# A recurrent integrator on one core: state in the units of the matrix sums, and a register as ScalarE's scale

## The chip, the cores and the metric

The kernel runs on one core of a Trainium2 chip. The metric is the device time of one execution in microseconds (us).

## The reference

An attention layer makes x (8 x 512 x 1024); then x drives a network of 1024 coupled neurons in 8 batches, integrated over 512 steps with four Runge-Kutta stages each. The output is x plus the trace of q.

```python
def derivative(q, p, drive, coupling, bias):
    dq = q - q ** 3 / 3.0 - p + drive + tanh(q) @ coupling.T + bias
    dp = EPSILON * (q + ALPHA - BETA * p)
# per step: dq1..dq4 at q, q + DT/2 dq1, q + DT/2 dq2, q + DT dq3
q_next = clip(q + DT / 6 * (dq1 + 2 * dq2 + 2 * dq3 + dq4), -20, 20)   # p likewise
trace[t] = q_next
x = x + attention(x);  x = x + trace(drive=x, q0=p0=cond)
```

The steps depend on one another, and within a step each stage needs tanh of the one before it, multiplied by the whole 1024 x 1024 matrix.

## The kernel before, in words

**Layout.** The 1024 neurons lie on 128 partitions in 8 blocks; a vector of the state is a tile of 128 x 64 (8 blocks of 8 batches). All tiles of the state are pieces of one buffer, `xb`, which held x for the attention before; so the profile calls them all `xb`. The drive, 512 slices of 64 columns, stays in SBUF as `drive` and is overwritten by the result.

**The matrix.** The setup finds the power of two `power` of the largest matrix entry, divides the matrix by it (times 2**14), and keeps it as two fp16 parts, `coup`. tanh, times 4096, is likewise split into two fp16 parts, `first` and `rest`, in `tanh_parts`. So TensorE's sums come out too large by a factor that is known only at run time, through `power`. The tile `step_scale` (128 x 4) holds, for each stage, the step length divided by that factor.

**One stage** (`stage`, for s = 0 to 3; 2048 in all) is cut into two chunks of blocks, chunk 0 with 24 columns and chunk 1 with 40. TensorE does 128 small matmuls (L619): 48 that need chunk 0 of tanh, then 40 and 40 that need chunk 1. The sums of chunk 0 are complete after 88 of them, those of chunk 1 at the end. VectorE turns the sums of each chunk by a transpose (L811: 96 columns wide for chunk 0, 160 for chunk 1). `q_of` (through `axpy`, L661) multiplies the turned sums of the `rest` part by `step_scale` and adds `base`: the next stage's q. ScalarE takes tanh of it (L437), and in stages 0 and 2 also makes the `first` part (L443); in stages 1 and 3 the `first` part was made earlier from a forecast (L449, L455). VectorE's `rest_of` makes the `rest` part. TensorE starts on a chunk when both of its parts are there.

**Beside that** VectorE prepares the next `base`: `with_first_part` adds the `first` sums, again times `step_scale`; ScalarE squares q (L481); `cubic_of` (L834) and `base_of` follow. Single instructions for p, for the forecasts and for the drive are put by hand between the others. In stage 3 VectorE clips p (`clip_p`, L927) and q (`clip_q`, L941), and `drive_less_p` (L936) forms the drive minus p; `look_ahead` (L932) has added the bias to the next drive slice between the first transpose and `q_of`. In stage 1 `drive_step` (L894) takes the difference of two drive slices; in stage 2 `trace` (L947) adds q to the drive slice of the step, which is the output.

**Order.** Each engine works through its list in order, and semaphores order the engines. VectorE's and ScalarE's loops have eight stages, two steps, in their body and run some 256 times; VectorE's closes behind a stage 0. SP stores the output every 32 steps. In the code, `STEP[s]` is the step length of stage s, and a scale given as `step_scale[:, s:s + 1]` is a pointer to one value for each partition, while a Python number is a constant within the instruction.

Of the kernel before, what the change touches and what calls it, by code (L numbers as in the profile page):

```python
# [18 lines left out]
P = 128  # L19
# [71 lines left out]
UNROLLED = 2  # L91
TANH_SCALE = 4096.0
COUP_EXP = 14
DRIVE_LOADS = 8
MATRICES = 4
# [4 lines left out]
def build(nc, x, x_pt, cond, cond_p, wq, wk, wv, wo, coupling_t, bias_p, out_pt):  # L100
    ctx = ExitStack()
    with ctx:
# [9 lines left out]

        drive = sb("drive", [P, T + 2, COLS])
        steps = drive[:, 1:1 + T, :]
# [41 lines left out]
        bias_sb = sb("bias_sb", [P, NC])  # L156
        step_scale = sb("step_scale", [P, STAGES])

        states = iter(range(0, KT * N, COLS))

        def state():

            first = next(states)
            return xb[:, :, :].rearrange("p c n -> p (c n)")[:, first:first + COLS]

        q_st = [state() for s in range(STAGES)]
        q_raw = state()
# [15 lines left out]
        bias_b = state()  # L183
        drive_b = state()
        drive_p = state()
# [163 lines left out]
        @block.gpsimd  # L349
        def _(pool):  # L350

            nc.gpsimd.memset(ident[:, :], 0.0).then_inc(pool_ready, 1)
            pool.wait_ge(pool_ready, 1)
            nc.gpsimd.memset(stack[:, :, :], 0.0).then_inc(pool_ready, 1)
            pool.wait_ge(pool_ready, 2)
            nc.gpsimd.affine_select(out=ident[:, :], in_=ident[:, :], compare_op=ALU.not_equal, fill=1.0,
                                    base=0, pattern=[[-1, P]], channel_multiplier=1).then_inc(pool_ready, 1)
            pool.wait_ge(pool_ready, 3)
            nc.gpsimd.affine_select(out=stack[:, :, :], in_=stack[:, :, :], compare_op=ALU.not_equal,
                                    fill=1.0, base=0, pattern=[[-DK, P // DK], [-1, DK]],  # L360
                                    channel_multiplier=1).then_inc(pool_ready, 1)
            fills = [(wo_sum[:, :], 0.0), (ones_row[:, :], 1.0), (head_t[:, :], 0.0),
                     (q_aug[:, :], 0.0), (k_aug[:, :], 0.0), (q_aug[DK:DK + 1, :], 1.0),
                     (drive[:, 0, :], 0.0), (drive[:, 1 + T, :], 0.0)]
# [6 lines left out]
        def _(act):  # L371
# [92 lines left out]
            for j in range(NCH):  # L464
                first_part_as_now(0, j, 1)
            nc.scalar.activation(square[:, :], q_st[0][:, :], ACT.Square).then_inc(square_ready, 1)
# [189 lines left out]
        def _(dve):  # L656
# [86 lines left out]
            for c in range(NC):  # L743
# [10 lines left out]

            V.tensor_scalar(all_max[:, :], small_ps[:, 0:1], 2.0 ** -100, 2.0 ** 100, ALU.max, ALU.min)\
             .then_inc(setup, 1)
# [11 lines left out]
            last.then_inc(setup, 1)  # L768

# [13 lines left out]


            V.memset(ps[:, 0:2 * NCH, :].rearrange("p a n -> p (a n)"), 0.0)
            V.memset(tanh_parts[:, 1, :, B * REST:B * (REST + 1)], 0.0).then_inc(start_ready, 1)
            V.tensor_copy(q_st[0][:, :], cond_sb[:, :, :].rearrange("p c b -> p (c b)"))
            V.tensor_scalar(p_st[:, :], cond_sb[:, :, :].rearrange("p c b -> p (c b)"), -SHIFT, None, ALU.add)
            V.memset(z[:, :], 0.0).then_inc(setup, 1)
            dve.wait_ge(setup, 5)  # L790
            for c in range(NC):
                last = V.tensor_scalar(cols(bias_b, (c, c + 1)), cols(z, (c, c + 1)), bias_sb[:, c:c + 1],
                                       -SHIFT, ALU.add, ALU.add)
# [5 lines left out]
            V.tensor_tensor(drive_b[:, :], steps[:, 0, :], bias_b[:, :], ALU.add).then_inc(setup, 1)  # L799
            dve.wait_ge(setup, 7)  # L800
            V.tensor_tensor(drive_p[:, :], drive_b[:, :], p_st[:, :], ALU.subtract).then_inc(setup, 1)

# [127 lines left out]
            def look_ahead(at):  # L930

                V.tensor_tensor(drive_b[:, :], drive_cols[:, bass.ds(at, COLS)], bias_b[:, :], ALU.add)  # L932

            def drive_less_p(now):
                dve.wait_ge(p_ready, now)
                V.tensor_tensor(drive_p[:, :], drive_b[:, :], p_st[:, :], ALU.subtract)\  # L936
# [12 lines left out]

            dve.wait_ge(setup, 8)  # L950
            z_of_first().then_inc(setup, 1)
# [8 lines left out]
            last.then_inc(start_turned, 1)  # L960
            dve.wait_ge(setup, 9)
            dve.wait_ge(start_turned, 1)
            with_first_part(0, z_first_part, z).then_inc(setup, 1)
            dve.wait_ge(setup, 10)
            base_of(0, 1)
            g0_of()


            def stage(s, now):

# [27 lines left out]
                if s == 1:  # L998
                    q_sum_r1()
                    drive_step_of((now + 2) * (COLS // STAGES))  # L1000
                if s == 2:
                    z_without_last(now)
                    trace((now - 3) * (COLS // STAGES))
                if s == 3:
                    clip_p()
                    clip_q(made)
                    drive_less_p(now)
                rest_of(parity, 1, made)
# [77 lines left out]
```

## Time and profile before

| | |
|---|---|
| median of three runs | 5930.74 us (5926.36 to 5930.91) |
| span of the profiled execution | 5929.8 us |
| TensorE matmul, weight load | 4508.3 us (76%), 3814.4 us (64%) |
| VectorE | 5526.4 us (93%), 31560 instructions |
| ScalarE | 2595.9 us (44%) |
| VectorE, `q_of` and `with_first_part` (L661 with `step_scale`) | 1601.2 us, 6145 instructions, mean 261 ns |
| ScalarE, tanh of a chunk (L437) | 940.7 us, 4098 instructions, mean 230 ns |

The span runs from the first to the last instruction of the profiled execution; the profile gives no other time for it. The recurrence begins near 428 us. Busy time of an engine counts an instruction from its start to its end, and on VectorE the next one starts before the end of the last; so two durations are told apart in what follows, how long an instruction takes, and how long it holds its engine (from its start to the next one's).

### The profile page before, as it was taken

To read this page: it belongs to the slowest core of one execution; us is meant where nothing else is said; L and a number is where in the kernel's file an instruction comes from. 1 tells how busy PE (TensorE), PEld (TensorE's weight loads), DVE (VectorE), ACT (ScalarE), POOL (GpSimd) and SP (SyncE) were. 2 spreads that over 40 slices of the span, in tenths; PEclk is the share of its full clock that TensorE was granted. 3 is DMA by queue.
4 is the path that set the end of the run, shared out by engine and by line. 5 is a ranking of instruction groups with operands and counts; after the bars stand their busy time and mean duration, and the time that the engine had idled before them with its cause. 6 is when DMAs were issued, how large, how long until landed. Compare 5 with 4: busy or idle time off the path is not lost.

```text
span 5929.8 us, 592455 instructions
## 1 busy us (share of the span) xinstructions
PE 4508.3 (76%) x263627; PEld 3814.4 (64%) x263627; DVE 5526.4 (93%) x31560; ACT 2595.9 (44%) x12040; POOL 5.6 (0%) x16
## 2 busy tenths in 40 slices
PE   7887777777777777777777777777777777777777
PEld 3446666666666666666666666666666666666666
DVE  6569999999999999999999999999999999999999
ACT  3334444444444444444444444444444444444444
POOL 0000000000000000000000000000000000000000
PEclk9999999999999999999999999999999999999999
DMA  5100000000000000000000000000000000000000
GB/s 211 45 16 0 0 7 0 7 0 7 0 0 7 0 7 0 7 0 0 7 0 7 0 7 0 0 7 0 7 0 7 0 0 7 0 7 0 7 0 7
DMA packets 11597, 57.06 MB, mean 10 GB/s; under 512 B 2616, under 2 KB 2616, under 8 KB 8512
## 3 DMA queue, kind: packets, MB, share of 16 engines
q1 hardware_dynamic: 11056, 55.84, 2.4%
q10 hardware_dynamic: 528, 1.05, 0.0%
q8 instruction: 7, 0.11, 0.0%
q14 instruction: 6, 0.05, 0.0%
HBM read 40.11 MB, written 16.78 MB: 10 GB/s over the span
## 4 chain that ended last, share of the span: by engine, by line
DVE 44%; PE 34%; issue 11%; ACT 10%; DMA 1%; DVEq 0%; SPq 0%; ACTq 0%
PE ps L619 29%; DVE xb L661 23%; DVE turned_sums L811 10%; ACT xb L437 7%; DVE tanh_parts L661 4%; ACT tanh_parts L443 3%; DVE xb L936 2%; DVE xb L834 2%; PE ps L508 1%; DVE xb L932 1%; DVE xb L927 1%; PE ps L563 1%; PE ps L526 1%; PE ps L552 1%; PE ps L542 1%
## 5 line engine op out<-in xcount | busy, mean ns | idle before, releaser
L619 PE MATMUL ps<-coup,tanh_parts 128*16 128x96 f16 (+1 forms) x262272 | 4159.4, 219 | 1345.7 <-DVE tanh_parts L661 680.6
L619 PEld LDWEIGHTS ps<-coup,tanh_parts 128*16 128x16 f16 x262272 | 3653.2, 89 | 1852.4 <-issue 863.9
L437 ACT ACTIVATE xb<-xb 128x24 f32<-128x24 f32 (+1 forms) x4098 | 940.7, 230 | 2968.7 <-DVE xb L661 2958.5
L661 DVE SCALAR_TENSOR_TENSOR xb<-xb 128x64 f32<-128x64 f32 x11267 | 2198.2, 214 | 17.7 <-issue 0.2
L661 DVE SCALAR_TENSOR_TENSOR xb<-turned_sums,step_scale,xb 128x64 f32<-128x64 f32 (+2 forms) x6145 | 1601.2, 261 | 16.2
L811 DVE STREAM_TRANSPOSE turned_sums<-ps 128x96 f32<-128x96 f32 (+1 forms) x4096 | 1284.2, 314 | 142.2 <-PE ps L619 67.3
L661 DVE SCALAR_TENSOR_TENSOR tanh_parts<-xb,tanh_parts 128x24 f16<-128x24 f32 (+1 forms) x4098 | 712.8, 174 | 49.9
L443 ACT ACTIVATE tanh_parts<-xb 128x24 f16<-128x24 f32 (+1 forms) x2050 | 470.9, 230 | 64.5
L481 ACT ACTIVATE xb<-xb 128x64 f32<-128x64 f32 x2048 | 498.8, 244 | 0.0
L834 DVE SCALAR_TENSOR_TENSOR xb<-xb 128x64 f32<-128x64 f32 x2049 | 445.6, 217 | 0.1
L455 ACT ACTIVATE tanh_parts<-xb 128x24 f16<-128x24 f32 (+1 forms) x2048 | 357.4, 221 | 32.1
L449 ACT ACTIVATE xb<-xb 128x64 f32<-128x64 f32 x1024 | 263.2, 257 | 0.0
L407 ACT ACTIVATE probs<-ps,neg_max 128x1024 f32<-128x1024 f32 x64 | 71.4, 1115 | 145.6 <-DVE neg_max L676 145.6
L508 PE MATMUL ps<-k_aug,q_aug 128*128 128x512 f32 x256 | 126.0, 616 | 0.0
L661 DVE SCALAR_TENSOR_TENSOR drive<-ps,row_scale,drive 128x512 f32 (+1 forms) x64 | 84.2, 1349 | 41.8 <-PE ps L552 40.6
L486 ACT ACTIVATE xb<-xb 128x64 f32<-128x64 f32 x512 | 122.8, 240 | 0.0
L676 DVE TENSOR_REDUCE neg_max<-ps 128x1 f32<-128x1024 f32 x64 | 78.2, 1223 | 45.7 <-PE ps L508 45.7
L936 DVE TENSOR_TENSOR xb<-xb 128x64 f32<-128x64 f32 x512 | 115.5, 226 | 0.0
L894 DVE TENSOR_TENSOR xb<-drive 128x64 f32 x512 | 111.4, 217 | 0.0
L870 DVE TENSOR_TENSOR xb<-xb 128x64 f32<-128x64 f32 x512 | 111.2, 217 | 0.0
L947 DVE TENSOR_TENSOR drive<-drive,xb 128x64 f32 x513 | 111.0, 216 | 0.0
L941 DVE TENSOR_SCALAR xb<-xb 128x64 f32<-128x64 f32 x512 | 99.6, 195 | 0.0
(68 smaller groups left out, 792.7 us busy)
## 6 DMA issues: line engine op xcount, KB each, us to landing
xb<-in_x SPq DMA_DIRECT2D x8, 2048.0 KB, 7.9
drive<-in_x_pt SPq DMA_DIRECT2D x8, 2048.0 KB, 24.6
out_pt<-drive SPq DMA_DIRECT2D x16, 1024.0 KB, 4.5
drive<-in_coupling_t SPq DMA_DIRECT2D x8, 512.0 KB, 11.5
mask_v<-in_cond SPq DMA_DIRECT2D x8, 132.0 KB
probs<-in_wo ACTq DMA_DIRECT2D x1, 1024.0 KB, 5.5
w_qkv<-in_wq SPq DMA_DIRECT2D x1, 64.0 KB, 3.8
w_qkv<-in_wk SPq DMA_DIRECT2D x1, 64.0 KB, 5.2
```

The source lines that it names most:

```text
L437: nc.scalar.activation(cols(tanh_sb, CHUNKS[j]), cols(q, CHUNKS[j]), ACT.Tanh)\
L443: nc.scalar.activation(tanh_part(parity, j, FIRST), by_block(tanh_sb, CHUNKS[j]), ACT.Copy, scale=TANH_SCALE).then_inc(first_ready[j], 1)
L449: nc.scalar.activation(tanh_hat[:, :], forecast[:, :], ACT.Tanh, scale=factor)\
L455: nc.scalar.activation(tanh_part(parity, j, FIRST), by_block(tanh_hat, CHUNKS[j]), ACT.Copy, scale=TANH_SCALE).then_inc(first_ready[j], 1)
L481: nc.scalar.activation(square[:, :], q_st[following][:, :], ACT.Square).then_inc(square_ready, 1)
L486: nc.scalar.activation(q_share[:, :], q_st[0][:, :], ACT.Copy, scale=Q_KEPT)\
L508: last = nc.tensor.matmul(score_ps[t % 2][:, BANK * h:BANK * (h + 1)], q_aug[:, P * t:P * (t + 1)], k_aug[:, BANK * h:BANK * (h + 1)], sta ...
L619: last = nc.tensor.matmul(product(s, j)[SQ * g:SQ * g + ROWS, :], tanh_parts[:, s % 2, k, :], coup[:, k, part, g, n0:n1, :].rearrange("p c ...
L661: return V.scalar_tensor_tensor(out=out, in0=a, scalar=factor, in1=c, op0=ALU.mult, op1=op1)
L811: V.transpose(turned_sums[:, CHUNKS[j][0]:CHUNKS[j][1], :].rearrange("p c r -> p (c r)"), product(s, j)).then_inc(product_turned[j], 1)
L834: V.scalar_tensor_tensor(out=cubic[:, :], in0=square[:, :], scalar=-3.0 if stage < 3 else OFFSET, in1=q_st[stage][:, :], op0=ALU.add, op1= ...
L936: V.tensor_tensor(drive_p[:, :], drive_b[:, :], p_st[:, :], ALU.subtract)\
```

## The change

The state q and p, the drive with bias, the clip bounds and all that is formed from them are kept divided by a unit, `power` times 2**-26, which is the size of 1 in TensorE's sums. The sums then enter with the step length alone, a constant in the instruction, and `step_scale` is gone. Where the state leaves these units, a factor known at run time stands in its place: ScalarE's tanh and square take `unit` as their scale, read once into a register; `look_ahead` and `trace` multiply by a pointer (`inv_unit`, `unit`), and `clip_p` and `clip_q` take their two bounds through pointers. The next drive is formed two steps ahead into one of two tiles, so that `drive_step` is a difference of tiles. `turned_sums` moves into `xb`. Cut to its core:

```diff
-TANH_SCALE = 4096.0
+TANH_EXP = 12
+TANH_SCALE = 2.0 ** TANH_EXP
+UNIT_EXP = TANH_EXP + COUP_EXP
+FORECASTS = [1.0, 1.5, 2.0]
...
-                nc.scalar.activation(cols(tanh_sb, CHUNKS[j]), cols(q, CHUNKS[j]), ACT.Tanh)\
+                nc.scalar.activation(cols(tanh_sb, CHUNKS[j]), cols(q, CHUNKS[j]), ACT.Tanh, scale=unit_of[1.0])\
...
-                nc.scalar.activation(tanh_hat[:, :], forecast[:, :], ACT.Tanh, scale=factor)\
+                nc.scalar.activation(tanh_hat[:, :], forecast[:, :], ACT.Tanh, scale=unit_of[factor])\
...
+            unit_of = {}
+            act.wait_ge(unit_ready, 1)
+            for i, factor in enumerate(FORECASTS):
+                unit_of[factor] = act.alloc_register(f"unit{i}")
+                act.load(unit_of[factor], unit[0:1, i:i + 1].bitcast(I32))
...
-                    nc.scalar.activation(square[:, :], q_st[following][:, :], ACT.Square).then_inc(square_ready, 1)
+                    nc.scalar.activation(square[:, :], q_st[following][:, :], ACT.Square, scale=unit_of[1.0]).then_inc(square_ready, 1)
...
-            for s in range(STAGES):
-                last = V.tensor_scalar(step_scale[:, s:s + 1], power[:, :], 2.0 ** -COUP_EXP,
-                                       STEP[s] / TANH_SCALE, ALU.mult, ALU.mult)
...
+            for i, factor in enumerate(FORECASTS):
+                last = V.tensor_scalar(unit[:, i:i + 1], power[:, :], factor * 2.0 ** -UNIT_EXP, None, ALU.mult)
+            last.then_inc(unit_ready, 1)
+            last = V.tensor_scalar(inv_unit[:, :], inv_power[:, :], 2.0 ** UNIT_EXP, None, ALU.mult)
+            for i, bound in enumerate([-CLAMP, CLAMP, -CLAMP - SHIFT, CLAMP - SHIFT]):
+                last = V.tensor_scalar(bounds[:, i:i + 1], inv_power[:, :], 2.0 ** UNIT_EXP, single(bound),
+                                       ALU.mult, ALU.mult)
...
-                axpy(by_block(out, CHUNKS[j]), turned_sum(j, REST), step_scale[:, s:s + 1],
+                axpy(by_block(out, CHUNKS[j]), turned_sum(j, REST), STEP[s],
...
-                return axpy(all_blocks(out), first_sums(), step_scale[:, stage:stage + 1], all_blocks(z_of_stage))
+                return axpy(all_blocks(out), first_sums(), STEP[stage], all_blocks(z_of_stage))
...
-            def drive_step_of(at):
-                V.tensor_tensor(drive_step[:, :], drive_cols[:, bass.ds(at + COLS, COLS)],
-                                drive_cols[:, bass.ds(at, COLS)], ALU.subtract)
+            def drive_step_of(now_at):
+                V.tensor_tensor(drive_step[:, :], drive_b[1 - now_at][:, :], drive_b[now_at][:, :], ALU.subtract)
...
-                V.tensor_scalar(p_st[:, :], p_raw[:, :], -CLAMP - SHIFT, CLAMP - SHIFT, ALU.max, ALU.min)\
+                V.tensor_scalar(p_st[:, :], p_raw[:, :], bounds[:, 2:3], bounds[:, 3:4], ALU.max, ALU.min)\
...
-                V.tensor_tensor(drive_b[:, :], drive_cols[:, bass.ds(at, COLS)], bias_b[:, :], ALU.add)
+                axpy(drive_b[into][:, :], drive_cols[:, bass.ds(at, COLS)], inv_unit[:, 0:1], bias_b[:, :])
...
-                V.tensor_scalar(q_st[0][:, :], q_raw[:, :], -CLAMP, CLAMP, ALU.max, ALU.min)\
+                V.tensor_scalar(q_st[0][:, :], q_raw[:, :], bounds[:, 0:1], bounds[:, 1:2], ALU.max, ALU.min)\
...
-                V.tensor_tensor(at, at, q_st[0][:, :], ALU.add).then_inc(traced, 1)
+                axpy(at, q_st[0][:, :], unit[:, 0:1], at).then_inc(traced, 1)
...
-                    look_ahead((now + STAGES) * (COLS // STAGES))
+                    look_ahead(now_at, (now + 2 * STAGES) * (COLS // STAGES))
```

## Rows read from the trace of the kernel before

**Rows 1.** Chain that ended last, by engine, share of the whole span (page).
```profile
DVE 44%; PE 34%; issue 11%; ACT 10%; DMA 1%; DVEq 0%; SPq 0%; ACTq 0%
```

**Rows 2.** Timeline of a stage 2: start us, us, engine, line, operation, tiles, count.
```profile
3001.21 0.35 DVE L811 STREAM_TRANSPOSE turned_sums<-ps 128x160 f32<-128x160 f32 x1
...
3001.48 0.15 DVE L661 SCALAR_TENSOR_TENSOR tanh_parts<-xb,tanh_parts 128x24 f16<-128x24 f32 x1
3001.59 0.26 DVE L661 SCALAR_TENSOR_TENSOR xb<-turned_sums,step_scale,xb 128x40 f32<-128x40 f32 x1
...
3001.77 2.02 PE L619 MATMUL ps<-coup,tanh_parts 128*16 128x96 f16 x128 [0.61 <-ACT tanh_parts L443]
3001.88 0.24 ACT L437 ACTIVATE xb<-xb 128x40 f32<-128x40 f32 x1 [0.22 <-DVE xb L661]
3001.90 0.22 DVE L947 TENSOR_TENSOR drive<-drive,xb 128x64 f32 x1
3002.15 0.24 ACT L443 ACTIVATE tanh_parts<-xb 128x40 f16<-128x40 f32 x1
...
3002.29 0.24 ACT L481 ACTIVATE xb<-xb 128x64 f32<-128x64 f32 x1
3002.41 0.28 DVE L661 SCALAR_TENSOR_TENSOR xb<-turned_sums,step_scale,xb 128x64 f32<-128x64 f32 x1
...
3002.60 0.22 DVE L834 SCALAR_TENSOR_TENSOR xb<-xb 128x64 f32<-128x64 f32 x1
3002.74 0.35 DVE L661 SCALAR_TENSOR_TENSOR xb<-xb 128x64 f32<-128x64 f32 x2
...
3003.15 0.28 DVE L811 STREAM_TRANSPOSE turned_sums<-ps 128x96 f32<-128x96 f32 x1
3003.36 0.18 DVE L932 TENSOR_TENSOR xb<-drive,xb 128x64 f32<-128x64 f32 x1
...
3003.84 0.35 DVE L811 STREAM_TRANSPOSE turned_sums<-ps 128x160 f32<-128x160 f32 x1
```

**Rows 3.** Windows, TensorE's weight loads: stretch, length, busy us (instructions), clock, DMA.
```profile
3002.41:3002.46 0.05, 0.00 (x0) 1.00 0.00 0
```

**Rows 4.** Timeline of VectorE in the stage 3 that follows.
```profile
3004.23 0.26 DVE L661 SCALAR_TENSOR_TENSOR xb<-turned_sums,step_scale,xb 128x40 f32<-128x40 f32 x1
3004.41 0.19 DVE L927 TENSOR_SCALAR xb<-xb 128x64 f32<-128x64 f32 x1
3004.52 0.19 DVE L941 TENSOR_SCALAR xb<-xb 128x64 f32<-128x64 f32 x1
3004.70 0.23 DVE L936 TENSOR_TENSOR xb<-xb 128x64 f32<-128x64 f32 x1
3004.84 0.19 DVE L661 SCALAR_TENSOR_TENSOR tanh_parts<-xb,tanh_parts 128x40 f16<-128x40 f32 x1
...
3005.89 0.27 DVE L811 STREAM_TRANSPOSE turned_sums<-ps 128x96 f32<-128x96 f32 x1
```

**Rows 5.** Timeline of VectorE at the branch of its loop, and the stage behind it.
```profile
3008.24 0.22 DVE L661 SCALAR_TENSOR_TENSOR xb<-xb 128x64 f32<-128x64 f32 x1
3008.72 0.28 DVE L811 STREAM_TRANSPOSE turned_sums<-ps 128x96 f32<-128x96 f32 x1 [0.26 <-PE ps L619]
...
3011.34 0.28 DVE L811 STREAM_TRANSPOSE turned_sums<-ps 128x96 f32<-128x96 f32 x1
```

**Rows 6.** Timeline of VectorE in the setup: constants alone, and one pointer.
```profile
28.04 0.33 DVE L766 TENSOR_SCALAR step_scale<-power 128x1 f32<-128x1 f32 x4
...
421.88 1.16 DVE L792 TENSOR_SCALAR xb<-xb,bias_sb 128x8 f32<-128x8 f32 x8
```

**Rows 7.** Groups of ScalarE by line and shape: busy us, mean ns, idle before.
```profile
L486 ACT ACTIVATE xb<-xb 128x64 f32<-128x64 f32 x512 | 122.8, 240 | 0.0
L407 ACT ACTIVATE probs<-ps,neg_max 128x1024 f32<-128x1024 f32 x64 | 71.4, 1115 | 145.6 <-DVE neg_max L676 145.6
...
L426 ACT ACTIVATE coup<-drive,coup_scale 128x256 f16<-128x256 f32 x32 | 12.9, 492 | 5.1 <-DVE coup_scale L763 5.1
```

More of the change, by code:

```diff
@@ L107, in sem @@
             return ctx.enter_context(nc.semaphore(name))
-        drive = sb("drive", [P, T + 2, COLS])
+        drive = sb("drive", [P, T + 3, COLS])
         steps = drive[:, 1:1 + T, :]
@@ L156, in build @@
         bias_sb = sb("bias_sb", [P, NC])
-        step_scale = sb("step_scale", [P, STAGES])
-        states = iter(range(0, KT * N, COLS))
+        xb_cols = xb[:, :, :].rearrange("p c n -> p (c n)")
+        turned_sums = xb_cols[:, 0:NC * SQ].rearrange("p (c r) -> p c r", r=SQ)
+        states = iter(range(NC * SQ, KT * N, COLS))
         def state():
             first = next(states)
-            return xb[:, :, :].rearrange("p c n -> p (c n)")[:, first:first + COLS]
+            return xb_cols[:, first:first + COLS]
+        units = state()
+        unit = units[:, 0:len(FORECASTS)]
+        inv_unit = units[:, 4:5]
+        bounds = units[:, 8:12]
         q_st = [state() for s in range(STAGES)]
@@ L183, in build @@
         bias_b = state()
-        drive_b = state()
+        drive_b = [state() for k in range(2)]
         drive_p = state()
@@ L223, in build @@
         scale_ready = sem("scale_ready")
+        unit_ready = sem("unit_ready")
         coup_high = sem("coup_high")
@@ L363, in _ @@
                      (q_aug[:, :], 0.0), (k_aug[:, :], 0.0), (q_aug[DK:DK + 1, :], 1.0),
-                     (drive[:, 0, :], 0.0), (drive[:, 1 + T, :], 0.0)]
+                     (drive[:, 0, :], 0.0), (drive[:, 1 + T:3 + T, :], 0.0)]
             for i, (buffer, value) in enumerate(fills):
@@ L465, in _ @@
                 first_part_as_now(0, j, 1)
-            nc.scalar.activation(square[:, :], q_st[0][:, :], ACT.Square).then_inc(square_ready, 1)
+            nc.scalar.activation(square[:, :], q_st[0][:, :], ACT.Square, scale=unit_of[1.0]).then_inc(square_ready, 1)
             with act.Fori(1, 1 + STAGES * STEPS, STAGES * UNROLLED) as now:
@@ L753, in _ @@
             dve.wait_ge(max_spread, 1)
-            V.tensor_scalar(all_max[:, :], small_ps[:, 0:1], 2.0 ** -100, 2.0 ** 100, ALU.max, ALU.min)\
+            V.tensor_scalar(all_max[:, :], small_ps[:, 0:1], 2.0 ** -64, 2.0 ** 100, ALU.max, ALU.min)\
              .then_inc(setup, 1)
@@ L764, in _ @@
              .then_inc(scale_ready, 1)
-            for s in range(STAGES):
-                last = V.tensor_scalar(step_scale[:, s:s + 1], power[:, :], 2.0 ** -COUP_EXP,
-                                       STEP[s] / TANH_SCALE, ALU.mult, ALU.mult)
-            last.then_inc(setup, 1)
             dve.wait_ge(scale_ready, 1)
@@ L781, in _ @@
             attend(B - 1, False)
+            for i, factor in enumerate(FORECASTS):
[5 more added lines that the diff above has]
+                                       ALU.mult, ALU.mult)
+            last.then_inc(setup, 1)
             V.memset(ps[:, 0:2 * NCH, :].rearrange("p a n -> p (a n)"), 0.0)
             V.memset(tanh_parts[:, 1, :, B * REST:B * (REST + 1)], 0.0).then_inc(start_ready, 1)
-            V.tensor_copy(q_st[0][:, :], cond_sb[:, :, :].rearrange("p c b -> p (c b)"))
-            V.tensor_scalar(p_st[:, :], cond_sb[:, :, :].rearrange("p c b -> p (c b)"), -SHIFT, None, ALU.add)
+            dve.wait_ge(setup, 4)
+            V.tensor_scalar(q_st[0][:, :], cond_sb[:, :, :].rearrange("p c b -> p (c b)"), inv_unit[:, 0:1], None,
+                            ALU.mult)
+            V.tensor_scalar(p_st[:, :], cond_sb[:, :, :].rearrange("p c b -> p (c b)"), -SHIFT, inv_unit[:, 0:1],
+                            ALU.add, ALU.mult)
             V.memset(z[:, :], 0.0).then_inc(setup, 1)
@@ L791, in _ @@
             for c in range(NC):
-                last = V.tensor_scalar(cols(bias_b, (c, c + 1)), cols(z, (c, c + 1)), bias_sb[:, c:c + 1],
+                last = V.tensor_scalar(cols(y, (c, c + 1)), cols(z, (c, c + 1)), bias_sb[:, c:c + 1],
                                        -SHIFT, ALU.add, ALU.add)
@@ L798, in _ @@
                 V.engine_nop().then_inc(q_next[j], 1)
-            V.tensor_tensor(drive_b[:, :], steps[:, 0, :], bias_b[:, :], ALU.add).then_inc(setup, 1)
+            V.tensor_scalar(bias_b[:, :], y[:, :], inv_unit[:, 0:1], None, ALU.mult).then_inc(setup, 1)
             dve.wait_ge(setup, 7)
-            V.tensor_tensor(drive_p[:, :], drive_b[:, :], p_st[:, :], ALU.subtract).then_inc(setup, 1)
+            axpy(drive_b[1][:, :], steps[:, 1, :], inv_unit[:, 0:1], bias_b[:, :])
+            axpy(drive_b[0][:, :], steps[:, 0, :], inv_unit[:, 0:1], bias_b[:, :]).then_inc(setup, 1)
+            dve.wait_ge(setup, 8)
+            V.tensor_tensor(drive_p[:, :], drive_b[0][:, :], p_st[:, :], ALU.subtract).then_inc(setup, 1)
             def turn_product(s, j, now):
@@ L926, in clip_p, with look_ahead, drive_less_p @@
             def clip_p():
-                V.tensor_scalar(p_st[:, :], p_raw[:, :], -CLAMP - SHIFT, CLAMP - SHIFT, ALU.max, ALU.min)\
+                V.tensor_scalar(p_st[:, :], p_raw[:, :], bounds[:, 2:3], bounds[:, 3:4], ALU.max, ALU.min)\
                  .then_inc(p_ready, STAGES)
-            def look_ahead(at):
-                V.tensor_tensor(drive_b[:, :], drive_cols[:, bass.ds(at, COLS)], bias_b[:, :], ALU.add)
-            def drive_less_p(now):
+            def look_ahead(into, at):
+                axpy(drive_b[into][:, :], drive_cols[:, bass.ds(at, COLS)], inv_unit[:, 0:1], bias_b[:, :])
+            def drive_less_p(now_at, now):
                 dve.wait_ge(p_ready, now)
-                V.tensor_tensor(drive_p[:, :], drive_b[:, :], p_st[:, :], ALU.subtract)\
+                V.tensor_tensor(drive_p[:, :], drive_b[now_at][:, :], p_st[:, :], ALU.subtract)\
                  .then_inc(drive_p_ready, STAGES)
@@ L946, in trace @@
                 at = drive_cols[:, bass.ds(at, COLS)]
-                V.tensor_tensor(at, at, q_st[0][:, :], ALU.add).then_inc(traced, 1)
-            dve.wait_ge(setup, 8)
+                axpy(at, q_st[0][:, :], unit[:, 0:1], at).then_inc(traced, 1)
+            dve.wait_ge(setup, 9)
             z_of_first().then_inc(setup, 1)
@@ L960, in _, with stage @@
             last.then_inc(start_turned, 1)
-            dve.wait_ge(setup, 9)
+            dve.wait_ge(setup, 10)
             dve.wait_ge(start_turned, 1)
             with_first_part(0, z_first_part, z).then_inc(setup, 1)
-            dve.wait_ge(setup, 10)
+            dve.wait_ge(setup, 11)
             base_of(0, 1)
             g0_of()
-            def stage(s, now):
+            def stage(s, now_at, now):
                 following = (s + 1) % STAGES
@@ L999, in stage @@
                     q_sum_r1()
-                    drive_step_of((now + 2) * (COLS // STAGES))
+                    drive_step_of(now_at)
                 if s == 2:
@@ L1006, in stage @@
                     clip_q(made)
-                    drive_less_p(now)
+                    drive_less_p(1 - now_at, now)
                 rest_of(parity, 1, made)
@@ L1041, in steps_until @@
                 return now // STAGES if isinstance(now, int) else dve.snap(now >> 2)
-            order = [(s + 1) % STAGES for s in range(STAGES)] * UNROLLED
-            stage(0, 1)
+            order = [((u + 1) % STAGES, (u + 1) // STAGES % 2) for u in range(STAGES * UNROLLED)]
+            stage(0, 0, 1)
             with dve.Fori(2, 2 + STAGES * (STEPS - UNROLLED), STAGES * UNROLLED) as now:
-                for s in order:
-                    now = stage(s, now)
+                for s, now_at in order:
+                    now = stage(s, now_at, now)
             now = 2 + STAGES * (STEPS - UNROLLED)
-            for s in order[:-1]:
-                now = stage(s, now)
+            for s, now_at in order[:-1]:
+                now = stage(s, now_at, now)
             trace(STEPS * COLS)
```

1 line of the change is left out of this document (removed).

## The prediction

> **What bounds the kernel now.** First the page's busy shares: VectorE works almost throughout, but TensorE is not far behind, so a busy share decides nothing. Then the chain of waits [rows 1]: it passes from TensorE to VectorE to ScalarE and back, so the time is the length of a loop of dependences run 2048 times (512 steps of four stages), and an instruction counts only if it lies on the loop. Then one stage in order of time [rows 2], read for what each start waits for. Last the two places where a stage differs: the tail of stage 3 [rows 4] and the branch of VectorE's loop, passed once in two steps [rows 5].
>
> In rows 2 a stage lasts 2.64 us, from one 160-wide transpose at 3001.21 to the next at 3003.84. The loop that sets it: transpose 3001.21; `q_of` of chunk 1 at 3001.59, taking 0.26; tanh at 3001.88, 0.03 after its end; first part at 3002.15, ending 3002.39; 0.10 later TensorE takes up the second 80 matmuls; it ends at 3001.77 + 2.02 = 3003.79; 0.05 later the next transpose. A second loop runs beside it: transpose 3001.21, `rest_of` of chunk 0 (3001.48 to 3001.63), TensorE's start at 3001.77, its 2.02, the next transpose. It is shorter only by the pause in the middle of TensorE's 128 matmuls: no weight load is in flight from 3002.41 to 3002.46 [rows 3], and with the restart that pause is 0.06. So the first loop can lose 0.06 a stage, and then both are equal. VectorE itself is not the limit in this stage: in front of the transpose at 3003.15 it is through with its list at about 3003.00 (two instructions from 3002.74, 0.14 apart).
>
> Stage 3 is otherwise. After `q_of` at 3004.23 it has `clip_p` 3004.41, `clip_q` 3004.52, `drive_less_p` 3004.70, and only then `rest_of` 3004.84; the next stage's transpose stands at 3005.89, 2.74 after this stage's own (3003.15), with no idle time noted before it [rows 2, 4]. And at the branch 0.48 passes from the last instruction to the transpose [rows 5], where 0.14 is usual, so stage 0 is bound there by VectorE's list too (one in two of its kind).
>
> **What an operand costs.** The change swaps kinds of operand, not counts of instructions. In rows 2 `with_first_part` (3002.41, a 128x1 scale from memory) holds VectorE for 0.19 to 0.20 and takes 0.28; the same operation and size with a constant holds it for 0.14 and takes 0.22 (3002.60 to 3002.74). So a scale from memory costs 0.06 in either count. The sums are also read in short runs; that the runs are not the cause is shown by the setup [rows 6]: eight TENSOR_SCALARs of contiguous operands with one pointer hold 0.134 each ((1.16 - 0.22) / 7), four with constants hold 0.06, of which seven more elements explain 0.007. A pointer there is 0.066 of holding, and 0.07 of duration.
>
> **Part by part.** (1) `q_of` and `with_first_part` take a constant: three instructions a stage lose 0.06 each. In the four stages of a pass of two steps that the loop of rows 2 binds (both stages 2, a stage 1, a stage 0), only `q_of` of chunk 1 is on it: 4 x 0.06 = 0.24 a pass. `q_of` of chunk 0 gives nothing there, since the transpose behind it waits for TensorE's end. In the stage 0 with the branch `q_of` of chunk 1 gives 0.06; of `with_first_part`'s 0.06 only 0.035 arrives, because `cubic_of` needs the square that ends at 3002.53, 0.07 before it, and a start follows its releaser by 0.03: 0.095. The stage 1 behind the branch (3008.72 to 3011.34 [rows 5]) starts with TensorE long done, so there `q_of` of both chunks count: 0.115 of 2 x 0.06, TensorE's matmuls being next. Sum 0.45 a pass.
>
> (2) Pointers come in at `look_ahead`, `trace`, `clip_p` and `clip_q`. `look_ahead` (3003.36 [rows 2]) becomes 0.06 longer in front of a `q_of` that is 0.06 shorter, and behind both the transpose waits for TensorE: nothing; without that cover 0.06 a step. `trace` (3001.90) stands before a wait for tanh, due about 0.06 earlier than 3002.15; 0.20 from 3001.84 still fits: nothing.
>
> (3) The clips get two pointers each, and are on the path of stage 3. No row shows an instruction with two. Both ends: the second free, so 0.066 each, or as dear as the first, so 0.13 each; that a pointer costs nothing at all I keep as the far end below, and nothing suggests a gain. I take 0.13: the nearest row is that of one pointer [rows 6], and a second operand at another address is a second one of the same. A clip with constants holds VectorE for about 0.094 (one element 0.06; 64 at one per ns would give 0.12 and more, above the 0.11 that rows 4 show with a wait in it, so two go at once, 0.033). Then, `q_of` being 0.06 shorter: `clip_p` 3004.35, `clip_q` 0.094 + 0.13 later at 3004.57, `drive_less_p` another 0.23 later at 3004.80, 0.10 behind its time in rows 4. The rest follows by 0.10, less 0.06 at `with_first_part`: stage 3 becomes 0.04 longer. With one price for both pointers `drive_less_p` moves 0.01, the stage 0.05 shorter; with free pointers 0.12 shorter. TensorE in this stage waits for the same `rest_of` and ends level with VectorE, so it adds nothing.
>
> (4) ScalarE's scale becomes a register in every tanh and square. No row has one. From below: a constant's price. From above: a pointer's. 256 elements with a pointer take 492 and 1024 take 1115, so 64 would take 336, against 240 with a constant [rows 7]: 96 ns. I take nothing: the waits of these instructions are against a register's count already, and a start still follows its releaser by 0.03 (3001.85 to 3001.88), so what an instruction has to look up is done before its wait ends.
>
> The Trainium skill says (ScalarE: Activation LUTs, What ACT_TABLE_LOAD costs) that each pointer operand adds about 93 ns to an ACTIVATE; the 96 agrees. Its "each" speaks for paying twice at the clips, if VectorE is alike, which no row shows.
>
> (5) `drive_step` reads two tiles in place of two slices: same instruction, in a gap. The setup gets eight small instructions (0.06 each [rows 6]), five or so longer or new: about 1 us in all. ScalarE's register loads stand beside VectorE's memsets; if each took a microsecond uncovered, 3 us. No wait is added inside the loop.
>
> Sum: a pass loses 0.45 and gets 2 x 0.04 back, 0.37; 256 passes give 95 us, the setup takes 1. The profiled span is 5929.8, the runs' median 5930.7, 0.9 around it; from the median: **5837 us**.
>
> **Rivals.** *One price for both pointers*: 0.45 + 0.10 = 0.55 a pass, 141 us: 5791. For it: two reads may overlap; against: nothing seen. With free pointers 0.69 a pass, 5755.
>
> *The register costs at every tanh* (the other side): if ScalarE looks it up after the wait has ended, each tanh of chunk 1 lies later on the loop of rows 2. At 0.095: four stages 0.38, the one behind the branch 0.15 (both tanhs), the branch stage 0.19 (tanh and square), together 0.72 less small cover in each, say 0.70 a pass or 180 us: 6017. It decides from 0.05 per ACTIVATE (0.37 / 0.70 x 0.095), where the gain is gone. Against it: the 0.03 above.
>
> *The 0.06 comes from the short runs, not from the pointer*: nothing is saved, `drive_less_p` comes 0.07 (one price) or 0.16 later, 2 x 256 times: 5967 to 6014. Against it rows 6, and `rest_of`, which reads and writes short runs in 0.15 (3001.48).
>
> *The operand's kind doesn't matter, the count does*: then nothing moves, 5931. The Trainium skill has this as advice (VectorE: DVE Perf Modes, Rules for kernel authors: minimise the count of instructions, not semaphores); by it the change, which removes none from a step, would do nothing. Rows 2 speak against that reading: 0.20 against 0.14 at equal size.
>
> **Numbers.** Forecast 0.42 (5815 to 5860 by itself); one price 0.30; free pointers 0.03; register at full or near full price 0.09, at a small price (0.02 to 0.05) 0.06, which lands at 5875 to 5931; short runs 0.04; count alone or a lost gain 0.06. The range 5772 to 5905 holds the first two and most of the small register price, some 0.79. A move under 0.2% (12 us) can't be told from none: faster 0.81, same 0.06, slower 0.13.
>
> **What would show it.** `q_of` of chunk 1 at 0.20 and `with_first_part` at 0.22; stages of 2.58 where 2.64 stood; no pause in TensorE's middle. Clips of 0.33 with 0.23 from start to start, `drive_less_p` 0.57 behind `q_of` (0.47 before) and stage 3 at 2.78; at 0.26 and 2.69 the one-price rival is right. Tanh of 40 elements still 237 ns, 0.03 after `q_of`: later or longer is the register's price. Wrong would be a stage 2 that stays at 2.64, or a branch that costs more than 0.48, since VectorE's program is laid out anew.

## The result, and the profile after

The changed kernel takes **5833.83 us** (median of four runs, 5832.71 to 5834.60) against 5930.14 (5926.36 to 5930.91): a ratio of 0.9839 (95% interval 0.9825 to 0.9853), 96 us less. The forecast was 5837, with a range from 5772 to 5905.

First the page of the kernel after: its span, the engines' busy time, and the chain that ended last, answering to [rows 1].

```profile
span 5832.2 us, 592464 instructions
PE 4466.0 (77%) x263627; PEld 3814.6 (65%) x263627; DVE 5405.9 (93%) x31566; ACT 2597.8 (45%) x12040; POOL 5.7 (0%) x16
DVE 48%; PE 33%; issue 16%; ACT 1%; DMA 1%; DVEq 0%; SPq 0%; ACTq 0%
```

VectorE has six instructions more and still works 93% of the span. In the chain ScalarE's share fell from 10% to 1%. That share does not stand for the first part of chunk 1: between 3000 and 3012 us of the kernel before, the chain's pieces on ScalarE are tanh and first part of chunk 0 and one tanh of chunk 1. What changed is the first part of chunk 0: in [rows 2] the start of the 128 matmuls is put down to ScalarE (`<-ACT tanh_parts L443`), in the timeline below to VectorE's `rest_of` (`<-DVE tanh_parts L675`). Before, the two came level, which the prediction did not note, and the faster `q_of` of chunk 0 brought ScalarE's forward; the start itself moved by only 0.007 (1.259 to 1.252 behind the 96-wide transpose, medians).

Next the timeline of a stage 2 and of the tail of the stage 3 behind it, answering to [rows 2, 4]: start, duration, engine, line, operation, tiles, count.

```profile
3009.10 0.35 DVE L835 STREAM_TRANSPOSE xb<-ps 128x160 f32<-128x160 f32 x1
...
3009.49 0.34 DVE L675 SCALAR_TENSOR_TENSOR xb<-xb 128x40 f32<-128x40 f32 x2
3009.63 1.79 PEld L633 LDWEIGHTS ps<-coup,tanh_parts 128*16 128x16 f16 x128 [0.79 <-ACT tanh_parts L452]
3009.66 1.97 PE L633 MATMUL ps<-coup,tanh_parts 128*16 128x96 f16 x128 [0.61 <-DVE tanh_parts L675]
3009.72 0.24 ACT L446 ACTIVATE xb<-xb 128x40 f32<-128x40 f32 x1 [0.23 <-DVE xb L675]
...
3009.99 0.24 ACT L452 ACTIVATE tanh_parts<-xb 128x40 f16<-128x40 f32 x1
...
3010.98 0.28 DVE L835 STREAM_TRANSPOSE xb<-ps 128x96 f32<-128x96 f32 x1
3011.19 0.24 DVE L675 SCALAR_TENSOR_TENSOR xb<-drive,xb 128x64 f32<-128x64 f32 x1
...
3011.68 0.35 DVE L835 STREAM_TRANSPOSE xb<-ps 128x160 f32<-128x160 f32 x1
3011.95 0.14 DVE L675 SCALAR_TENSOR_TENSOR tanh_parts<-xb,tanh_parts 128x24 f16<-128x24 f32 x1
3012.06 0.20 DVE L675 SCALAR_TENSOR_TENSOR xb<-xb 128x40 f32<-128x40 f32 x1
3012.18 0.31 DVE L950 TENSOR_SCALAR xb<-xb 128x64 f32<-128x64 f32 x1
3012.20 0.67 PEld L633 LDWEIGHTS ps<-coup,tanh_parts 128*16 128x16 f16 x48 [0.79 <-issue]
...
3012.40 0.31 DVE L964 TENSOR_SCALAR xb<-xb 128x64 f32<-128x64 f32 x1
3012.62 0.21 DVE L959 TENSOR_TENSOR xb<-xb 128x64 f32<-128x64 f32 x1
3012.76 0.19 DVE L675 SCALAR_TENSOR_TENSOR tanh_parts<-xb,tanh_parts 128x40 f16<-128x40 f32 x1
...
3013.75 0.28 DVE L835 STREAM_TRANSPOSE xb<-ps 128x96 f32<-128x96 f32 x1
```

From 160-wide transpose to 160-wide transpose it is now 2.58 (3009.10 to 3011.68), where 2.63 stood. The first part ends at 3009.99 + 0.24 = 3010.23; with the 0.10 of [rows 2] TensorE can take up chunk 1 at 3010.33. It is busy with chunk 0 until then: 48 weight loads take 0.67 (3012.20, in the next stage), from 3009.66 on that is 3010.33 too. So the two loops are level, and the matmuls take 1.97 (2.02 before). The window of weight loads around that moment, which was empty in [rows 3], is full:

```profile
3010.30:3010.35 0.05, 0.05 (x5) 1.00 0.00 0
```

From the start of the 48th matmul to that of the 49th, 0.107 to 0.115 passed in all stages but 3 before, and 0.053 to 0.059 after (medians over all passes); so the pause of about 0.06 is gone. `q_of` of chunk 1 takes 0.20 (3012.06). In the tail the clips take 0.31 and follow each other by 0.22; `drive_less_p` stands 0.56 behind `q_of`, and the stage lasts 2.77 (3010.98 to 3013.75). Then the branch, answering to [rows 5]:

```profile
3005.43 0.22 DVE L675 SCALAR_TENSOR_TENSOR xb<-xb 128x64 f32<-128x64 f32 x1
3005.91 0.28 DVE L835 STREAM_TRANSPOSE xb<-ps 128x96 f32<-128x96 f32 x1 [0.26 <-PE ps L633]
...
3008.41 0.28 DVE L835 STREAM_TRANSPOSE xb<-ps 128x96 f32<-128x96 f32 x1
```

The branch costs 0.48 as before; the stage 1 behind it lasts 2.50, where 2.62 stood.

For the whole run I take the length of a stage as the distance between starts of 96-wide transposes, the median over all passes (a pass is two steps, eight stages; the letters are the two halves of a pass, and a is the half behind the branch). The runs e2 to e11 are told below. In ns:

| stage | before | after | q_of 0 pointer (e2) | memsets (e10) | pointer without memsets (e11) | order (e8) |
|---|---|---|---|---|---|---|
| 0, with branch | 2822 | 2744 | 2743 | 2743 | 2743 | 2749 |
| 1a | 2629 | 2506 | 2580 | 2509 | 2581 | 2509 |
| 2a | 2637 | 2575 | 2579 | 2575 | 2579 | 2575 |
| 3a | 2744 | 2767 | 2867 | 2870 | 2772 | 2602 |
| 0, other | 2622 | 2569 | 2572 | 2502 | 2573 | 2574 |
| 1b | 2637 | 2574 | 2580 | 2575 | 2579 | 2574 |
| 2b | 2634 | 2574 | 2580 | 2575 | 2580 | 2574 |
| 3b | 2744 | 2768 | 2768 | 2772 | 2768 | 2602 |
| pass (mean) | 21467 | 21078 | 21267 | 21122 | 21177 | 20759 |

A pass lost 389 ns; 256 passes make 99.6 us, a little more than the 96 that the time fell.

### The profile page after: what moved, and what is told of

The parts are those of the page before. It is cut to its first block, busy times and chain, and to the rows that moved or that the text cites. A ratio compares the mean times of both kernels' runs of the same rounds, so it can differ in the third digit from the quotient of the medians.

```text
span 5832.2 us, 592464 instructions
## 1 busy us (share of the span) xinstructions
PE 4466.0 (77%) x263627; PEld 3814.6 (65%) x263627; DVE 5405.9 (93%) x31566; ACT 2597.8 (45%) x12040; POOL 5.7 (0%) x16
## 4 chain that ended last, share of the span: by engine, by line
DVE 48%; PE 33%; issue 16%; ACT 1%; DMA 1%; DVEq 0%; SPq 0%; ACTq 0%
PE ps L633 29%; DVE xb L675 24%; DVE xb L835 10%; DVE tanh_parts L675 6%; DVE xb L858 2%; DVE xb L950 2%; DVE xb L959 2%; PE ps L522 1%; ACT xb L446 1%; PE ps L577 1%; PE ps L540 1%; PE ps L556 1%; PE ps L566 1%; DVE drive L675 1%; DVE xb L964 1%
## 5 line engine op out<-in xcount | busy, mean ns | idle before, releaser
L675 DVE SCALAR_TENSOR_TENSOR xb<-xb 128x64 f32<-128x64 f32 (+2 forms) x17412 | 2998.8, 209 | 17.6
L835 DVE STREAM_TRANSPOSE xb<-ps 128x96 f32<-128x96 f32 (+1 forms) x4096 | 1291.3, 315 | 198.0 <-PE ps L633 67.5
L675 DVE SCALAR_TENSOR_TENSOR tanh_parts<-xb,tanh_parts 128x24 f16<-128x24 f32 (+1 forms) x4098 | 697.9, 170 | 32.1
L858 DVE SCALAR_TENSOR_TENSOR xb<-xb 128x64 f32<-128x64 f32 x2049 | 452.9, 221 | 0.0
L964 DVE TENSOR_SCALAR xb<-xb 128x64 f32<-128x64 f32 x512 | 157.7, 308 | 0.0
L950 DVE TENSOR_SCALAR xb<-xb 128x64 f32<-128x64 f32 x512 | 157.7, 308 | 0.0
L675 DVE SCALAR_TENSOR_TENSOR drive<-xb,drive 128x64 f32 x513 | 141.4, 276 | 0.0
L675 DVE SCALAR_TENSOR_TENSOR xb<-drive,xb 128x64 f32<-128x64 f32 x514 | 125.2, 244 | 0.0
L675 DVE SCALAR_TENSOR_TENSOR drive<-ps,row_scale,drive 128x512 f32 (+1 forms) x64 | 84.1, 1348 | 41.9 <-PE ps L566 40.5
```

The source lines that it names most:

```text
L675: return V.scalar_tensor_tensor(out=out, in0=a, scalar=factor, in1=c, op0=ALU.mult, op1=op1)
L835: V.transpose(turned_sums[:, CHUNKS[j][0]:CHUNKS[j][1], :].rearrange("p c r -> p (c r)"), product(s, j)).then_inc(product_turned[j], 1)
L858: V.scalar_tensor_tensor(out=cubic[:, :], in0=square[:, :], scalar=-3.0 if stage < 3 else OFFSET, in1=q_st[stage][:, :], op0=ALU.add, op1= ...
L950: V.tensor_scalar(p_st[:, :], p_raw[:, :], bounds[:, 2:3], bounds[:, 3:4], ALU.max, ALU.min)\
L964: V.tensor_scalar(q_st[0][:, :], q_raw[:, :], bounds[:, 0:1], bounds[:, 1:2], ALU.max, ALU.min)\
```

## The experiments

All are the kernel after with one edit; their ratios are against runs of the kernel before on the same chip. The differences to the kernel after are differences of medians across chips; the kernel before came out between 5930.1 and 5935.2 beside these runs, so some us of a difference can be the chip's. My theory was that a scale from memory holds VectorE 0.06 longer, and that this counts only on the loop of dependences. The main rival was the count: VectorE is busy 93% of the time, so what shortens 2048 of its instructions by 0.06 should be worth 125 us wherever they stand.

**One pointer put back at a time (e1, e2, e3).**

```diff
+            for s in range(STAGES):
+                V.memset(step_ptr[:, s:s + 1], STEP[s])
...
-                axpy(by_block(out, CHUNKS[j]), turned_sum(j, REST), STEP[s],
+                axpy(by_block(out, CHUNKS[j]), turned_sum(j, REST), step_ptr[:, s:s + 1] if j == 1 else STEP[s],
```

That is e1; e2 has `j == 0`, and e3 has `step_ptr` in `with_first_part` instead.

> Only q_of of chunk 1 takes its step from memory again (a 128x1 tile filled with the same constants); everything else is as in the kernel after. My theory (0.061 us of holding and of duration for the pointer, and it counts where the instruction is on the loop of dependences): all eight stages of a pass become 0.06 longer, 0.48 us a pass, 256 passes, +123 us: 5957. By the count of busy time (each of 2048 instructions 0.061 longer): +125, so this run alone does not tell them apart; it is the one with which the next two are compared. If the short runs of the turned sums were the cause and not the pointer: no change, 5834.

Measured 5963.0 (ratio 1.0052, 1.0036 to 1.0069): +129 on the kernel after. Some 11 of it are likely a stall that is told below (an estimate from e10).

> Only q_of of chunk 0 takes its step from memory again: the same 2048 pointers as for chunk 1, 0.061 us each. My theory: in front of the second transpose VectorE waits for TensorE's end in seven of eight stages, so only the stage 1 behind the branch grows, by 0.06: +16 us, 5850. By the count of busy time: +125, 5959.

Measured 5880.9 (0.9916, 0.9899 to 0.9933): +47. A miss for both theories.

> Only with_first_part takes its step from memory again (2048 times, 0.061 us). My theory: stage 3 grows by 0.06 (twice a pass), but the stage 0 behind it, where TensorE has then had more time, gives 0.06 of it back once and 0.02 the other time: net 0.04 a pass, +10 us, 5844 (up to 0.12 a pass, +31 us, 5865, if stage 0 gives nothing back). By the count of busy time: +125, 5959.

Measured 5863.8 (0.9886, 0.9870 to 0.9903): +30. Both stages 3 grew by 0.06, one by another 0.1; the stages 0 behind them gave back 0.069 (2500 for 2569) and 0.033 (2711 for 2744).

The same 2048 pointers cost 129, 47 and 30 us, by place. Groups of VectorE by line and shape, first of after, then of e2 (busy us, mean ns, idle before):

```profile
L675 DVE SCALAR_TENSOR_TENSOR xb<-xb 128x24 f32<-128x24 f32 x2048 | 375.2, 183 | 0.0
```

```profile
L676 DVE SCALAR_TENSOR_TENSOR xb<-xb 128x24 f32<-128x24 f32 x2048 | 499.1, 244 | 12.2
```

The instructions are 124 us longer in sum, and the run 47. So the count is refuted; but 47 is not 16 either. The table has both reasons for e2: stage 1a grew by 0.074 (0.061 was expected; the instruction with the pointer also starts 0.010 later behind the semaphore wait in front of it, 0.076 instead of 0.066), which is 19 us, and one stage 3 of two grew by 0.1, which nothing in the edit explains. The same stage is longer in e1 (2928, where 3b has 2829) and e3 (2928 and 2830). What the three have in common beside the pointer is four memsets in VectorE's setup.

**The stall of 0.1 us (e10, e11).**

```diff
+            for s in range(STAGES):
+                V.memset(step_ptr[:, s:s + 1], STEP[s])
```

> The kernel after with four memsets of 128x1 more in VectorE's setup, into a tile that nothing reads; the loop is the same instruction for instruction. The three runs with a pointer had these four, and in each of them one stage 3 in two was 0.099 us longer, in front of z_of_first. If the place of the loop in VectorE's program makes that stall: 256 times 0.099, +25 us, 5859. If the pointers make it: 5834.

Measured 5845.4 (0.9848, 0.9832 to 0.9864): 12 us over the kernel after by the medians, though the kernel before came out 5 us higher beside it (5935.2) than beside the kernel after; by the pass of the table +44 ns, 11 us. The stall is there. Timelines of VectorE in e10, the stage 3b and the stage 3a, from `rest_of` on:

```profile
3004.46 0.19 DVE L676 SCALAR_TENSOR_TENSOR tanh_parts<-xb,tanh_parts 128x40 f16<-128x40 f32 x1
3004.64 0.50 DVE L676 SCALAR_TENSOR_TENSOR xb<-xb 128x64 f32<-128x64 f32 x3
```

```profile
3015.06 0.19 DVE L676 SCALAR_TENSOR_TENSOR tanh_parts<-xb,tanh_parts 128x40 f16<-128x40 f32 x1
3015.34 0.49 DVE L676 SCALAR_TENSOR_TENSOR xb<-xb 128x64 f32<-128x64 f32 x3
```

From `rest_of` to `z_of_first` it is 0.18 in the one and 0.28 in the other, the same two instructions with the same operands; 0.187 and 0.284 as medians over all passes. I had priced the stall at 25 us. It came to 11, because the stage 0 behind a longer stage 3 finds TensorE further on and gives 0.067 back (2502 for 2569).

> q_of of chunk 0 with its step from memory, as in the run e2, but the tile is filled by GpSimd, so that VectorE's program has as many instructions as in the kernel after. If the place of the loop makes the stall of 0.099: it is gone, and the pointer costs only the 0.074 us of the stage 1 behind the branch and some 0.005 in the others, +23 us, 5857. If the pointer makes the stall: 5881. By the count of busy time, +125: 5959.

```diff
+            fills += [(step_ptr[:, s:s + 1], STEP[s]) for s in range(STAGES)]
```

Measured 5860.6 (0.9874, 0.9857 to 0.9890): +27. Stage 3a lasts 2772 again, 1a 2581: the pointer alone costs 99 ns a pass, 25 us. With the four instructions gone from VectorE's program the stall is gone, and with them alone it is there: it comes with four more instructions in front of the loop, not with the operand. That they make it by shifting the loop's place in the program is argued; no run moved the loop by another number of instructions.

**The clips (e4, e5).**

```diff
-                V.tensor_scalar(p_st[:, :], p_raw[:, :], bounds[:, 2:3], bounds[:, 3:4], ALU.max, ALU.min)\
+                V.tensor_scalar(p_st[:, :], p_raw[:, :], bounds[:, 2:3], single((CLAMP - SHIFT) * 2.0 ** 31), ALU.max, ALU.min)\
```

That is `clip_p` in e5, `clip_q` likewise; in e4 the lower bound is a constant too.

> clip_p and clip_q take both bounds as constants, in the unit that this input gives (2**-31). My theory (two pointers at 0.066 each in each clip, 0.13 a clip): stage 3 falls from 2.77 to about 2.62, where TensorE becomes the limit: 0.16 twice a pass, -82 us, 5752. If two pointers cost one price of 0.066: -0.13 less cover, -46, 5788.

Measured 5758.2 (0.9707, 0.9691 to 0.9723): -76, stage 3 at 2622.

> Each clip has its lower bound through a pointer and its upper bound as a constant in the unit of this input. My theory (each pointer has its own price, 0.066 of holding and 0.07 of duration): from the start of clip_p to that of clip_q 0.16 us (0.224 with two), clips of 0.25 (0.308 with two), stage 3 0.09 shorter, -46 us: 5788. One price for any number of pointers: everything stays, 0.224, 0.308, 5834. If only the second pointer is dear: 0.12 and 0.19, -82 us, 5752.

Measured 5787.1 (0.9756, 0.9739 to 0.9772): -47, stage 3 at 2684. Timelines of the clips in e4, then in e5:

```profile
3010.19 0.20 DVE L675 SCALAR_TENSOR_TENSOR xb<-xb 128x40 f32<-128x40 f32 x1
3010.31 0.19 DVE L950 TENSOR_SCALAR xb<-xb 128x64 f32<-128x64 f32 x1
3010.43 0.20 DVE L964 TENSOR_SCALAR xb<-xb 128x64 f32<-128x64 f32 x1
3010.60 0.23 DVE L959 TENSOR_TENSOR xb<-xb 128x64 f32<-128x64 f32 x1
```

```profile
3008.68 0.20 DVE L675 SCALAR_TENSOR_TENSOR xb<-xb 128x40 f32<-128x40 f32 x1
3008.80 0.25 DVE L950 TENSOR_SCALAR xb<-xb 128x64 f32<-128x64 f32 x1
3008.97 0.25 DVE L964 TENSOR_SCALAR xb<-xb 128x64 f32<-128x64 f32 x1
3009.15 0.23 DVE L959 TENSOR_TENSOR xb<-xb 128x64 f32<-128x64 f32 x1
```

`clip_q` takes 195, 247 and 308 ns with no, one and two pointers: 52 for the first, 61 for the second. One price for both is refuted. In e4 stage 3 lost 0.146, where I had 0.16; so 76 and not 82. I had also expected TensorE to become the limit there, and it does not: 2622, where the stages that it binds last some 2574. In both runs `drive_less_p` starts 0.10 behind the end of `clip_p`, for which it waits (3010.50 to 3010.60, 3009.05 to 3009.15). So between e5 and e4 a pointer counts through the duration of `clip_p` alone, 0.061; in the kernel after `drive_less_p` follows the two holds of 0.22.

**ScalarE's scale (e6, e7).**

```diff
-                unit_of[factor] = act.alloc_register(f"unit{i}")
-                act.load(unit_of[factor], unit[0:1, i:i + 1].bitcast(I32))
+                unit_of[factor] = unit[:, i:i + 1]
```

In e7 the line is `unit_of[factor] = factor * 2.0 ** -31`.

> ScalarE's tanh and square take their scale through a pointer to unit in place of the register. My theory: an ACTIVATE with a pointer is 0.095 us longer (492 - (1115 - 492) / 4, scaled to 64 elements, gave 336 against 240), and tanh of chunk 1 is on the loop nearly everywhere: 0.72 us a pass, +184 us, 6018. If ScalarE fetches the pointer's value before its wait ends, as it seems to do with the register: 5834. If the pointer is fetched once for all elements beside the fixed start: 5834 to 5880.

Measured 6007.8 (1.0128, 1.0111 to 1.0145): +174, slower than the kernel before.

> ScalarE's scale is a constant in the instruction, with the unit of this input (2**-31); the three register loads stay out. My theory: the register costs nothing at the path, so the time stays, 5834, and tanh of 40 columns stays 0.236, 0.034 behind q_of. If the register has a small price of 0.01 to 0.03 that the comparison with before has hidden: 0.08 to 0.23 a pass less, 5775 to 5814.

Measured 5833.1 (0.9831, 0.9815 to 0.9848): the same as after. Tanh of 40 columns, groups by line and shape, in after, e7 and e6:

```profile
L446 ACT ACTIVATE xb<-xb 128x40 f32<-128x40 f32 x2049 | 484.0, 236 | 707.0 <-DVE xb L675 707.0
```

```profile
L446 ACT ACTIVATE xb<-xb 128x40 f32<-128x40 f32 x2049 | 483.9, 236 | 708.3 <-DVE xb L674 708.3
```

```profile
L446 ACT ACTIVATE xb<-xb 128x40 f32<-128x40 f32 x2049 | 671.3, 328 | 530.9 <-DVE xb L674 392.0
```

With a register and with a constant the instruction takes the same 236 ns, and the run the same time (5833.8 and 5833.1 us); the pointer costs 92 ns in each instruction. The Trainium skill (ScalarE: Activation LUTs, What ACT_TABLE_LOAD costs) has 93 for a pointer, which agrees with the 92; of a register it says nothing.

**A better order (e8, e9).** The clips cost what they cost because three instructions stand in a row between `q_of` of chunk 1 and `rest_of`. `clip_p` can go ahead of the second transpose, where VectorE waits for TensorE, if `look_ahead` makes room for it. In short:

```diff
                 if s == 3:
-                    look_ahead(now_at, (now + 2 * STAGES) * (COLS // STAGES))
+                    p_next()
                 q_of(s, 0, now)
...
                 if s == 3:
-                    p_next()
+                    clip_p(now)
                 turn_product(s, 1, now)
...
-                    clip_p()
-                    clip_q(made)
                     drive_less_p(1 - now_at, now)
+                    clip_q(made)
...
+                    look_ahead(now_at, (now + 2 + 2 * STAGES) * (COLS // STAGES))
```

The last line stands at the end of stage 1; `p_sum_q3` moves ahead of `with_first_part` in stage 2, `clip_p` waits for `p_next` by a semaphore of its own, and `z_of_first` waits for `clip_q`. e9 has the same order and `UNROLLED = 4`.

> All operands as after; only VectorE's order in stage 3 is changed: p_next stands in look_ahead's place, clip_p in front of the second transpose, behind q_of of chunk 1 come drive_less_p and then clip_q; look_ahead goes to the end of stage 1, p_sum_q3 ahead of with_first_part in stage 2. The number of instructions and of pointers is that of the kernel after. My theory (stage 3 is longer only because clip_p, clip_q and drive_less_p stand in a row on the path): stage 3 falls from 2.77 to 2.59, level with TensorE, twice a pass, -93 us, 5741. If the pointers count by their number and not by their place: 5834. If look_ahead at the end of stage 1 delays the transpose of stage 2 by its 0.2, twice a pass: half or all of the gain is lost, 5741 to 5843.

Measured **5751.3** (0.9696, 0.9679 to 0.9712): 83 us below the kernel after, with the same operands. VectorE in a stage 3 of e8:

```profile
3010.93 0.28 DVE L836 STREAM_TRANSPOSE xb<-ps 128x96 f32<-128x96 f32 x1
...
3011.43 0.32 DVE L952 TENSOR_SCALAR xb<-xb 128x64 f32<-128x64 f32 x1
3011.66 0.34 DVE L836 STREAM_TRANSPOSE xb<-ps 128x160 f32<-128x160 f32 x1
...
3012.03 0.20 DVE L676 SCALAR_TENSOR_TENSOR xb<-xb 128x40 f32<-128x40 f32 x1
3012.15 0.22 DVE L961 TENSOR_TENSOR xb<-xb 128x64 f32<-128x64 f32 x1
3012.29 0.31 DVE L966 TENSOR_SCALAR xb<-xb 128x64 f32<-128x64 f32 x1
3012.54 0.20 DVE L676 SCALAR_TENSOR_TENSOR tanh_parts<-xb,tanh_parts 128x40 f16<-128x40 f32 x1
...
3013.53 0.28 DVE L836 STREAM_TRANSPOSE xb<-ps 128x96 f32<-128x96 f32 x1
```

`rest_of` stands 0.51 behind `q_of` (0.70 in after, 3012.06 to 3012.76), and `clip_p` fills what was a wait for TensorE in front of the second transpose. It overfills it a little: that transpose stands 0.73 behind the first, 0.70 in after, so stage 3 is 2602, where the stages that TensorE binds last 2574. `look_ahead` at the end of stage 1 delayed nothing: 1a and 1b last 2509 and 2574 (2506 and 2574 in after).

> The order of the run before (clip_p ahead of the second transpose, look_ahead in stage 1) and four steps in a loop body in place of two, on every engine. My theory: the branch makes its stage 0 2.749 instead of 2.574, 0.175 us; it is passed 128 times less, -22 us from 5751: 5729. If a body of twice the length brings stalls of its own, such as the 0.1 us that one of the two stages 3 showed where VectorE's setup had four instructions more: 5729 plus 13 for each (128 times 0.1).

Measured 5740.7 (0.9670, 0.9654 to 0.9686): 11 us below e8, half of what I expected. A stage 0 with the branch is 0.17 longer than another (2746 against 2575), but the stage 1 behind it is 0.067 shorter (2508 against 2575), since TensorE has gone on meanwhile; so an avoided branch is worth 0.10, and 128 of them 13 us. The expectation had left out what stage 1 gives back. No stage of e9 showed the stall.

## Why the prediction was right, point by point

- *A scale from memory costs 0.06.* Right: `q_of` went from 260 to 199 and from 244 to 183 ns, `with_first_part` from 278 to 217, and e1 to e3 bring it back, in one instruction at a time. The short runs of the turned sums, the third rival, are still there and are not its cause.
- *Four stages of a pass lose 0.06, through `q_of` of chunk 1 alone.* Right for both stages 2 and 1b, 0.060 to 0.063; the other stage 0 lost 0.053. That TensorE's pause goes shows in the window without a break and in the 1.97. That chunk 0 is covered there e11 shows: its pointer costs 0.004 to 0.006 in these stages, although there the profile puts TensorE's start down to ScalarE's first part of chunk 0 again, in two stages of four.
- *Stage 0 with the branch, 0.095.* Too large: 0.078. `with_first_part` holds VectorE 0.034 less, as worked out, because `cubic_of` waits for the square; but the second transpose waits for TensorE now, so that `q_of` of chunk 1 starts 0.009 later in its stage, and `cubic_of` holds 0.007 longer.
- *Stage 1 behind the branch, 0.115.* 0.123, but not in two equal parts: TensorE's start came 0.071 earlier, through `q_of` of chunk 0 (0.061, and 0.010 less behind its wait), and the pause in TensorE's middle gave 0.054.
- *Stage 3, +0.04.* +0.024. What decided the size, that two pointers cost twice, was an assumption from one row of a single pointer; e5 shows that it holds. The two terms under it were both a little off: I had 0.094 for a clip with constants and 0.066 for a pointer. e5's one pointer holds 163 ns and after's two 223, 60 for the second; taken off once more, 103 are left for a clip without one, an estimate, since in e4 `clip_q` waits for `q_of` and hides it. The errors cancel at 0.224, by luck. `drive_less_p` came 0.095 later; but it no longer had to wait for `clip_p`, and held 0.135 instead of 0.143. So what follows came 0.087 later, less 0.06 at `with_first_part`. It is this shortened wait that the 0.04 lacked.
- *The register costs nothing.* Right: e7 is the proof, and e6 the measure of what the rival's mechanism would have cost: 6008, against the 6017 given.
- *`look_ahead` and `trace` cost nothing.* Right in the run: `look_ahead` takes 0.24 instead of 0.18, and the second transpose stands as far behind the first as before (692 and 694 ns); `trace` stands in both stages 2, which last as long as 1b (2575, 2574 and 2574).
- *Setup, 1 us.* Not settled: the first transpose of the start came between 426 and 432 us in the runs, whatever the edit, so a difference of one or two microseconds can't be read from one profile each.
- *The sum.* 0.37 a pass, measured 0.389: stage 3 paid 0.03 less than forecast over its two places, and the stage with the branch and the one behind it together gave 0.01 less.

The rival of the count failed in both its forms: VectorE has more instructions and the time fell; and 2048 times the same 0.06 cost from 27 us (e11) to 129 us (e1, the stall included).

## What to carry to other kernels

Where an instruction has a scale or a bound that is known only at run time, look at which kind of operand brings it and where the instruction stands: on VectorE each pointer cost 0.05 to 0.06 us here, on ScalarE 0.09, and a register on ScalarE nothing. Changing the units so that the pointers move from instructions on the loop to covered ones was worth 96 us; moving the instructions that then carry the pointers to where their engine waits (e8) another 83, at the same operands. And price a gain on one stage with the next stage in view: three times here (e3, e9, e10) the stage behind gave back, or took, 0.07.

## What the runs showed of the hardware that was not expected

A stall of 0.098 us stands at one place of VectorE's loop, between a semaphore wait and the instruction behind it, in one of two copies of the same instructions, when four instructions more precede the loop; the copy half a pass (10.6 us) away has none. What is waited for, `drive_less_p`, has ended 0.21 us before that instruction starts (0.11 in the other copy). It is a cost of an edit that the edit's own instructions don't show, and a reason to compare stage by stage: e2 without that look would have put 20 us too much on a pointer. The Trainium skill (Runtime: NRT & Kernel Launch, Instruction fetch mechanics) says that instructions are fetched in blocks and that crossing from one to the next is mostly hidden; no run here shows where a block ends. But e10's trace has no DMA packet at all from 3000 to 3100 us, where the stall comes once in each pass of 21 us:

```profile
DMA packets 0, 0.00 MB, mean 0 GB/s; under 512 B 0, under 2 KB 0, under 8 KB 0
```

So it is not a fetch through a DMA queue that the trace records; what else makes it stays open.
